# A sine by polynomial on GpSimd, and VectorE's steps around the first two scans in a written order

## The chip, the cores and the metric

The kernel runs on one core of a Trainium2 chip: TensorE (PE in the rows), VectorE (DVE), ScalarE (ACT), GpSimd (POOL) and the SyncE queue (SP) that issues the loads. The metric is the device time of one execution in microseconds (us); the median of three executions counts.

## What is computed

A two-layer block over `x` of 16 sequences of 256 tokens and 256 features. Layer 0 is a layer norm, a diagonal complex recurrence (32 states) over time, and a GELU perceptron whose output gates it:

```python
mag, theta = exp(-exp(softplus(nu_log))), exp(theta_log)
A = mag * (cos(theta) + i sin(theta)); gamma = sqrt(1 - mag * mag)
h[t] = A * h[t-1] + gamma * (B @ xn[t])            # complex, 32 states
s = Re(C @ h) + D * xn
g = silu(proj2 @ gelu(proj1 @ xn + b1) + b2)       # 256 -> 1024 -> 256
x = x + s * g
```

Layer 1 is causal attention with a low-rank key and value path and 16 heads, gated by a mixture of LoRA experts. The change lies in layer 0 alone.

## The kernel before

Layer 0 takes the tokens in eight chunks of 512 (`NC = 8`, chunk `c`). The five engines have programs of their own, written as loops over 70 steps `g` (`L0_STEPS`), and what stands in a step is a hand-written table of step numbers; semaphores alone order one engine against another. A step of TensorE has one up block, hidden block `g`: `l0_up` (six products of 512 columns into one of two banks `fbank`), and the down block of two steps before, `l0_down(g-2)` (twelve products of 256 columns). Numbers are split in a high and a low part, so every product stands three times (`three`, line 537). Between lie, once in a chunk: `l0_turn` (transposes of the normed input `xn`, two halves), `l0_bu` (the recurrence's input), and `l0_y(c, b)` (line 597, the product of the states `Z[b]` with the matrix `RR`).

ScalarE does the high parts: `x_high`, `w1_high`, `w2_high`, `b_high`, and in each step `l0_gelu` (gelu of the bank into `hs`, then a rounded copy `hh`). VectorE does the low parts (`x_low`, `w1_low`, `w2_low`, `b_low`, and `h_low`, which writes `hl`), the layer norm (`l0_stats`, `l0_normed`; the first two chunks' roots too, `l0_norm`), the size of the decay (`magnitude`, a chain of one-column steps handed out by `go(make, 7)`), and `scan(c)`: the input is turned by tables `tci`, `tsi` (four steps), summed, scanned in time, and turned back by `tc`, `tsn` (the two halves of `CS`) into `Z[0]` and `Z[1]`. `states_out` adds the product of `l0_y` to the skip path, `l0_sum` and `l0_gate` make the gate, `l0_out` writes `x`.

GpSimd makes the tables: it exponentiates `theta_log`, reduces eight angles (1, 2, 4 ... 128 times theta), gives them halved to ScalarE (semaphore `ang`), which takes the sine (`angles`), then fixes the pairs to length one and doubles the table `CS` eight times. It then scales `RR`, `tci` and `tsi`, fills the small tables `rope_c`, `rope_s`, and takes the roots of later chunks (`l0_roots`) and two products on weights of layer 1 (`weigh_factors`, line 1951).

The places the change touches: ScalarE's start (lines 1079 to 1128), where an up block's gelu stands behind three `w1_high` and `angles`; TensorE's `l0_up(0)` and the tables of `l0_bu`, `l0_turn`, `l0_y` (lines 807 to 845); VectorE's loop (lines 1653 to 1756); GpSimd's table maker (lines 1866 to 1915).

Of the kernel before, what the change touches and what calls it, by code (L numbers as in the profile page):

```python
# [59 lines left out]
PRODUCT_AT = 5  # L60
L0_STEPS = 70
# [11 lines left out]
    "w1h", "w2h", "bh", "xth", "gelu", "hsh", "sin", "th0", "wrh", "wnh", "wmh", "lbh", "woh",  # L73
    "yth", "mi", "kt", "qn", "gx", "mt", "th1", "p", "oth",
# [5 lines left out]
    "gated", "clean", "par", "ang", "nu", "tab", "rt", "fill", "rl", "lr", "kr", "kvr", "n", "qq", "nw", "rs", "oc", "kwk", "kwv",  # L80
# [110 lines left out]
def build(nc, x, consts, rows, vecs, w1t, w2t, b1c, bt, ct, nuth, wqn, wkbt, wqr, wkva, wvbt, wo,  # L191
          baset, lorab, loraa, routert, out):
    ctx = ExitStack()
    with ctx:
# [60 lines left out]
        pari = sb("pari", [128, 4], I32, l0)  # L255
        st0 = sb("st0", [128, 4, 6], F32, l0)
# [95 lines left out]
        top = lg[:, 96:112].rearrange("p (t x) -> p t x", t=2)  # L352

# [178 lines left out]
        def _(e):  # L532
# [24 lines left out]

            def l0_up(c, hb):
# [38 lines left out]
            def l0_y(c, b):  # L597
                w.wait_ge("zz", 2 * c + b + 1)
# [191 lines left out]
            for g in range(L0_STEPS):  # L790
# [43 lines left out]
                c, r = divmod(g - 4, 8)  # L834
                if r == 0 and 0 <= c < NC - 1:
                    l0_turn(c + 1, 0)
# [6 lines left out]
                if g in (11, 16, 23, 31, 39, 47, 55, 63):  # L843
                    c = (11, 16, 23, 31, 39, 47, 55, 63).index(g)
                    l0_y(c, 1)
# [51 lines left out]
        def _(e):  # L897
# [39 lines left out]
            def angles():  # L937
                w.wait_ge("ang", 1)
                w.wait_ge("sin", 1)
                e.activation(col(48, 16), col(32, 16), ACT.Sin).then_inc(SEM["sin"], 1)  # L940
# [6 lines left out]
            def rope_high():  # L947
                w.wait_ge("wqr", 16)
                for k in range(2):
                    e.activation(wq_hi[:, k, :, 128:256], wrs[:, k, :, :], ACT.Copy,  # L950
                                 scale=-SCALE).then_inc(SEM["wrh"], 1)
# [128 lines left out]
            e.activation(col(56), tsn[:, 0:1], ACT.Sin).then_inc(SEM["sin"], 1)  # L1080
# [3 lines left out]
            for g in range(L0_STEPS):  # L1084
                c, r = divmod(g - 10, 8)
                if r == 0 and 0 <= c < NC:
                    l0_tanh(c, 0)
                c, r = divmod(g - 10, 8)
                if r == 0 and 0 <= c < NC:
# [7 lines left out]
                if g == 3:  # L1097
                    b_high()
                if g == 0:
                    w1_high(1)  # L1100
                if g == 0:
                    w1_high(2)
                if g == 0:
                    w1_high(3)
# [4 lines left out]
                if g == 0:  # L1109
                    angles()  # L1110
                if g == 1:
                    w2_high(0)
                if g == 2:
                    w2_high(1)
                if g == 3:
                    w2_high(2)
                if g == 5:
                    w2_high(3)
# [8 lines left out]
                if g == 11:  # L1127
                    rope_high()
                if g == 64:
                    weighed(0)  # L1130
                if g < 8 * NC:
                    l0_gelu(g)
                if g == 54:
# [12 lines left out]
                c, r = divmod(g - 4, 8)  # L1146
                if r == 0 and 0 <= c < NC - 1:
# [60 lines left out]
        def _(e):  # L1208
# [30 lines left out]
            def l0_stats(c):  # L1239
                w.wait_ge(f"x{c}", 16)  # L1240
                w.wait_ge("xn", c)
                for i in range(4):
                    if c == 0 and i == 2:
                        w.wait_ge("x0b", 16)
                    j = e.bn_stats(st0[:, i, :], X[:, 4 * c + i, :])
                j.then_inc(SEM["bn"], 1)
                took("bn")
                for i in range(4):
                    j = e.bn_aggr(mv0[:, i, :], st0[:, i, :])
# [3 lines left out]
            def l0_normed(c):  # L1253
                if c > 1:
                    w.wait_ge("rl", c - 1)
                w.wait_ge("xo", 2 * (c - 2))
                for i in range(4):
                    j = e.tensor_scalar(xn[c % 3][:, i, :], X[:, 4 * c + i, :], mv0[:, i, 0:1], rs0[:, 4, i:i + 1],
# [13 lines left out]
            def magnitude():  # L1272
# [40 lines left out]
                e.tensor_tensor(gamma, gamma, t[:, 4, :], ALU.mult).then_inc(SEM["mag"], 1)  # L1313
# [43 lines left out]
            def scan(c):  # L1357

                w.wait_ge("bu", c + 1)
                w.wait_ge("tab", 3)  # L1360
# [61 lines left out]
            def rope_low():  # L1422
                for k in range(2):
                    w.wait_ge("wrh", k + 1)
                    e.scalar_tensor_tensor(wq_lo[:, k, :, 128:256], wrs[:, k, :, :], -SCALE,
                                           wq_hi[:, k, :, 128:256].bitcast(F32), ALU.mult,
                                           ALU.subtract).then_inc(SEM["wrl"], 1)
# [224 lines left out]
            gate = norm = make = iter(())  # L1652
            for g in range(L0_STEPS):
                c, r = divmod(g - 3, 8)
                if r == 0 and 1 <= c < NC - 1:
                    l0_normed(c + 1)
                c, r = divmod(g - 0, 8)
# [5 lines left out]
                if g == 1:  # L1663
                    w2_low(0)
                if g == 2:
                    w2_low(1)
                if g == 3:
                    w2_low(2)
                if g == 6:
                    w2_low(3)  # L1670
                if g == 58:
                    l1_kv(0)
                if g in (7, 13, 21, 29, 37, 45, 53, 61):
                    c = (7, 13, 21, 29, 37, 45, 53, 61).index(g)
                    skip(c, 0)
                if g in (10, 16, 23, 31, 39, 47, 55, 63):
                    c = (10, 16, 23, 31, 39, 47, 55, 63).index(g)
                    skip(c, 1)
                if g == 0:
                    w1_low(1)  # L1680
                if g == 0:
                    w1_low(2)
                if g == 0:
                    w1_low(3)
                if g in (9, 12, 20, 28, 36, 44, 52, 60):
                    c = (9, 12, 20, 28, 36, 44, 52, 60).index(g)
# [13 lines left out]
                if g == 11:  # L1700
                    rope_low()
# [13 lines left out]
                if g == 4:  # L1715
# [4 lines left out]
                if g == 4:  # L1720
# [473 lines left out]
```

## Time and profile before

| What | us |
|---|---|
| median of three executions (796.82 to 797.35) | 797.14 |
| the profiled execution's own time | 797.71 |
| its span | 795.9 |
| PE busy in the span | 780.1 |
| DVE busy | 682.7 |
| ACT busy | 524.0 |
| POOL busy | 477.1 |

The span is the time from the first to the last instruction on the core; the profiled execution's own time is 1.8 us more. Busy time is a sum over the whole span. A stretch of TensorE's busy time can be at either of its two granted clocks (1.2 or 2.4 GHz), which the rows by stretch give as a share of the higher (PEclk).

### The profile page before, as it was taken

The numbers are of one execution on the slowest core, as the hardware profiler recorded it, in microseconds if no ns is written. First come the engines' busy times: TensorE is split into PE (matmuls) and PEld (weight loads), VectorE is DVE, ScalarE is ACT, GpSimd is POOL, SyncE is SP. The second block draws the span as 40 slices with busy tenths as digits, with TensorE's granted clock in tenths as the row PEclk, the third lists the DMA queues.
The fourth block names the chain that finished last, engine by engine and source line by source line (L and its number), as shares of the span: only waits on it lengthen the run. The fifth ranks groups of instructions, "written<-read, shape, count | busy, mean of one in ns | idle before, by whom it ended". The sixth has DMA issues, their size and how long they took to land.

```text
span 795.9 us, 23134 instructions
## 1 busy us (share of the span) xinstructions
PE 780.1 (98%) x7976; PEld 712.7 (90%) x7976; DVE 682.7 (86%) x2615; ACT 524.0 (66%) x1612; POOL 477.1 (60%) x1261
## 2 busy tenths in 40 slices
PE   7999999999999999999999999999999999999988
PEld 5888888888889889899988999999899998999867
DVE  6898797887788799899898998988899998999885
ACT  4554455455563787777767777777777767777682
POOL 6833022022334687776868677686776868668673
PEclk8999999999999999999999999999999999999999
DMA  8600011000001322232222322222232222322120
GB/s 297 251 20 18 1 68 67 1 1 1 1 12 33 55 46 44 55 63 39 52 39 44 56 54 54 38 47 46 54 65 34 49 42 50 57 47 52 33 52 28
DMA packets 101334, 41.15 MB, mean 52 GB/s; under 512 B 91744, under 2 KB 98400, under 8 KB 100576
## 3 DMA queue, kind: packets, MB, share of 16 engines
q1 hardware_dynamic: 98896, 38.89, 21.9%
q8 instruction: 63, 1.03, 0.5%
q10 hardware_dynamic: 2320, 0.79, 0.4%
q14 instruction: 55, 0.45, 0.2%
HBM read 14.47 MB, written 4.19 MB: 23 GB/s over the span
## 4 chain that ended last, share of the span: by engine, by line
PE 88%; DVE 5%; POOL 2%; issue 2%; ACT 2%; ACTq 0%; DMA 0%; POOLq 0%; DVEq 0%
PE bank L537 61%; PE bank L745 11%; PE bank L767 8%; PE bank L738 3%; PE bank L601 1%; POOL par L1822 1%; DVE SM L1583 1%; PE bank L653 1%; ACT SM L1036 1%; PE bank L554 1%; DVE PT L1606 1%; PE bank L613 1%; PE bank L627 1%; POOL SM L1989 1%; PE bank L672 0%
## 5 line engine op out<-in xcount | busy, mean ns | idle before, releaser
L1036 ACT ACTIVATE SM<-SM,stb 128x224 f32<-128x224 f32 (+7 forms) x512 | 206.1, 405 | 63.4 <-DVE stb L1583 58.9
L1989 POOL TENSOR_SCALAR SM<-SM,stb 128x224 f32<-128x224 f32 (+7 forms) x512 | 196.1, 402 | 67.0 <-DVE stb L1590 65.5
L537 PE MATMUL bank<-yh,wq_lo 128*128 128x256 f32 x512 | 150.5, 294 | 0.0
L537 PE MATMUL bank<-yh,wq_hi 128*128 128x256 f32 x512 | 144.6, 282 | 0.0
L537 PE MATMUL bank<-yl,wq_hi 128*128 128x256 f32 x512 | 144.6, 282 | 0.0
L745 PE MATMUL bank<-KT,QT 128*128 128x192 f32 (+4 forms) x640 | 120.9, 327 | 1.7 <-DVE stb L1583 1.7
L1583 DVE CUSTOM_DVE_ANT_0 SM<-bank,CONST 128x224 f32<-128x224 f32 (+3 forms) x320 | 96.9, 346 | 24.1 <-PE bank L745 21.3
L1606 DVE STREAM_TRANSPOSE PT<-SM 128x128 f32<-128x128 f32 (+2 forms) x232 | 99.4, 460 | 16.2 <-PE bank L767 16.2
L745 PEld LDWEIGHTS bank<-KT,QT 128*128 128x128 f32 x640 | 97.5, 190 | 5.3 <-DVE stb L1583 3.6
L537 PEld LDWEIGHTS bank<-yh,wq_lo 128*128 128x128 f32 x512 | 97.0, 190 | 1.4
L537 PEld LDWEIGHTS bank<-yh,wq_hi 128*128 128x128 f32 x512 | 97.0, 190 | 0.0
L537 PEld LDWEIGHTS bank<-yl,wq_hi 128*128 128x128 f32 x512 | 97.0, 189 | 0.0
L1036 ACT ACTIVATION_READ_ACCUMULATOR SM<-SM,stb 128x1 f32 x512 | 96.1, 188 | 0.0
L921 ACT ACTIVATE hs<-bank,B 128x512 f32<-128x512 f32 x64 | 43.9, 686 | 74.1 <-PE bank L537 68.6
L1982 POOL TENSOR_TENSOR QA<-QA 128x256 f32<-128x256 f32 x62 | 46.3, 746 | 58.5 <-DVE QA L1554 58.5
L1008 ACT ACTIVATE QT<-bank 64x512 f32<-64x512 f32 x128 | 75.4, 589 | 6.5 <-PE bank L537 4.8
L1554 DVE TENSOR_TENSOR QA<-bank,TR 128x512 f32<-128x512 f32 x124 | 79.3, 682 | 0.2
L537 PE MATMUL bank<-woe_hi,ol 128*128 128x256 f32 x256 | 75.4, 294 | 0.7 <-issue 0.7
L537 PE MATMUL bank<-w2h,hl 128*128 128x256 f32 x256 | 74.4, 291 | 0.0
L537 PE MATMUL bank<-w2l,hh 128*128 128x256 f32 x256 | 72.4, 283 | 0.0
L537 PE MATMUL bank<-w2h,hh 128*128 128x256 f32 x256 | 72.4, 283 | 0.0
L537 PE MATMUL bank<-woe_hi,oh 128*128 128x256 f32 x256 | 72.1, 281 | 0.0
(218 smaller groups left out, 2068.9 us busy)
## 6 DMA issues: line engine op xcount, KB each, us to landing
QT<-QA SPq DMA_DIRECT2D x240, 64.0 KB, 2.1
PT<-KV SPq DMA_DIRECT2D x256, 16.0 KB, 1.8
out<-fo SPq DMA_DIRECT2D x32, 128.0 KB, 2.0
X<-in_x SPq DMA_DIRECT2D x7, 512.0 KB, 11.2
stage<-in_wqn SPq DMA_DIRECT2D x2, 1024.0 KB, 9.2
stage<-in_wo SPq DMA_DIRECT2D x2, 1024.0 KB, 5.0
stage<-in_w1t SPq DMA_DIRECT2D x4, 256.0 KB, 5.6
stage<-in_w2t SPq DMA_DIRECT2D x2, 512.0 KB, 7.6
```

The source lines that it names most:

```text
L537: i = e.matmul(dst, a, b, start=(first and j == 0), stop=(last and j == 2), skip_group_check=skip)
L738: j = e.matmul(sbank[n % 2][32 * i:32 * i + 32, at:to], KT[b % 3][:, p, 32 * kb:32 * kb + 32], Q[:, :, kb:3, i, :], start=True, stop=True)
L745: j = e.matmul(sbank[n % 2][:, at], Q[:, q, :, :].rearrange("p h c -> p (h c)"), KT[b % 3][:, p, 0:32 * q + 32], start=True, stop=True)
L767: j = e.matmul(sums[64 * half:64 * half + 64, :, 32 * q:32 * end], C[rows_, kb // 2, at], PT[rows_, 2 * half:2 * half + 2, kb, q:end, :], ...
L921: e.activation(hs[g % 2][:, :], fbank[g % 2][:, :], ACT.Gelu, bias=B1[:, g % 8:g % 8 + 1]).then_inc(SEM["gelu"], 1)
L1008: i = e.activation(QT[r, (2 * b + g // 2) % 3, p, :, g % 2:4:2, :].rearrange("p n j c -> p j n c"), src[r, :, :, :], ACT.Copy)
L1036: i = e.activation(M[:, at], M[:, at], ACT.Exp, bias=S[:, 0, j:j + 1], scale=-1.0, accum_out=S[:, 1, j:j + 1])
L1554: i = e.tensor_tensor(A[:, part, :, :, g % 2, :], src, TR[:, part, :].rearrange("p (n c) -> p n c", n=8).unsqueeze(1).broadcast_to([128, 2 ...
L1583: i = e.tensor_tensor_reduce(M[:, at], bk[:, at], mask[:, 224 - 32 * q:256], 1.0, 3e38, ALU.add, ALU.min, S[:, 0, j:j + 1])
L1606: return e.transpose(PT[:, slot, 0:k, q:q + some, :].rearrange("p k q c -> p q k c"), src)
L1982: e.tensor_tensor(A[:, 0, 0, :, :], A[:, 0, 0, :, :], A[:, 1, 1, :, :], ALU.subtract)
L1989: i = e.tensor_scalar(P[:, at], P[:, at], S[:, 2, j:j + 1], 1.0, ALU.mult, ALU.mult)
```

## The change

It does six things. (1) ScalarE no longer takes the sine. GpSimd evaluates sine and cosine of the half angles by polynomials of the squared angle, two of eight columns at once, in 15 instructions where it had nine, and without a wait for ScalarE; ScalarE's first instruction is a gelu of one column instead of a sine. (2) `w1_high` and `w1_low` of parts 1 to 3 are spread over steps (0, 2, 4 on ScalarE, 0, 2, 5 on VectorE) instead of standing all in step 0; `w2_low`, `b_high`, `b_low` move by a step or two. (3) TensorE's first up block takes its products with the input's high part first and those with the low part last. (4) ScalarE makes `tci` and `tsi` after gelu 10; GpSimd's `rope` tables move behind the roots of chunk 2. (5) VectorE's steps 10 to 18 are written out in one function, and the steps of TensorE for the first two chunks' states move: `l0_bu(0)` from step 5 to 7 and `l0_bu(1)` from 12 to 14, `l0_y` from steps 10, 11, 14, 16 to 12, 13, 16, 17, all four behind the down block. (6) Chunk 3's statistics use layer 1's small buffers, so that they can be taken in step 10 (before: 16); `rope_high` and `rope_low` are split, and the latter moves from step 11 to 20 and 22.

```diff
+TURN_FIRST = (5, 13, 20, 28, 36, 44, 52)
+BU_AT = (7, 14, 20, 28, 36, 44, 52, 60)
+SCAN_AT = (10, 14, 20, 28, 36, 44, 52, 60)
+Y_AHEAD = {8 * c + 6: c for c in range(2, NC)}
+Y_BEHIND = {12: (0, 0), 13: (0, 1), 16: (1, 0), 17: (1, 1), **{8 * c + 7: (c, 1) for c in range(2, NC)}}
...
+            def l0_first():
+                sl = slice(0, 128)
...
+                for k in range(2):
+                    w.wait_ge("xth", k + 1)
+                    e.matmul(fbank[0][:, :], w1l[:, k, sl], xh[0][:, k, :], start=(k == 0), stop=False)
+                    e.matmul(fbank[0][:, :], w1h[:, k, sl], xh[0][:, k, :], start=False, stop=False)
+                for k in range(2):
+                    w.wait_ge("xtl", k + 1)
+                    i = e.matmul(fbank[0][:, :], w1h[:, k, sl], xl[0][:, k, :], start=False, stop=(k == 1))
...
+            def rotated_tables():
+                w.wait_ge("cs", 1)
+                w.wait_ge("mag", 1)
+                e.activation(tci[:, :], tc, ACT.Copy, scale=col(6)).then_inc(SEM["tab"], 1)
+                e.activation(tsi[:, :], tsn, ACT.Copy, scale=col(7)).then_inc(SEM["tab"], 1)
...
-            e.activation(col(56), tsn[:, 0:1], ACT.Sin).then_inc(SEM["sin"], 1)
+            e.activation(trig[:, 15, 0:1], tsn[:, 0:1], ACT.Gelu)
...
+            def first_steps(g):
+                if g == 10:
+                    l0_stats(3)
+                if g in (12, 13, 16, 18):
+                    states_out(*{12: (0, 0), 13: (0, 1), 16: (1, 0), 18: (1, 1)}[g])
+                if g == 14:
+                    l0_gate(0, 1)
+                if g == 17:
+                    l0_sum(1)
+                h_low(g)
+                if g == 10:
+                    go(make)
+                    scan(0)
+                if g == 11:
+                    l0_normed(2)
...
+                if g == 13:
+                    l0_gate(0, 0)
+                    x_low(2, 0)
+                if g == 14:
+                    x_low(2, 1)
+                    scan(1)
...
-            w.wait_ge("sin", 2)
-            tt(c8, c8, c8, ALU.mult)
...
+            ts(ab, r8, 0.5, None, ALU.mult)
+            both = ab.unsqueeze(1).broadcast_to([128, 2, 8])
+            tt(q1.rearrange("p (i n) -> p i n", i=2), both, both, ALU.mult)
+            tt(SUMS[:, 0:3, :], ODD, q1.unsqueeze(1).broadcast_to([128, 3, 16]), ALU.mult)
...
+            e.tensor_tensor(CS[:, :, 128:256], CS[:, :, 128:256], G[:, :, 0:128], ALU.add).then_inc(SEM["cs"], 1)
```

ScalarE at its start, before (`xh0` is the input's high part, `hs` and `hh` the gelu's output and its rounded copy, `stage` the loaded weights):

```order
L1080 ACT_TABLE_LOAD
L1080 ACTIVATE par<-CS 128x1 [waits par]
L903 ACTIVATE w1h<-stage0 128x2x256 [waits wu0]
L914 ACTIVATE xh0<-bank 128x512 [waits tx] x2
L903 ACTIVATE w1h<-stage0 128x2x256 [waits wu1]
L903 ACTIVATE w1h<-stage0 128x2x256 [waits wu2]
L903 ACTIVATE w1h<-stage0 128x2x256 [waits wu3]
L940 ACTIVATE par<-par 128x16 [waits sin,ang]
L921 ACT_TABLE_LOAD [waits b1]
L921 ACTIVATE hs0<-bank,B1 128x512 [waits f1]
```

The same place in the change:

```order
L1109 ACT_TABLE_LOAD
L1109 ACTIVATE trig<-CS 128x1 [waits par]
L932 ACTIVATE w1h<-stage0 128x2x256 [waits wu0]
L943 ACTIVATE xh0<-bank 128x512 [waits tx] x2
L932 ACTIVATE w1h<-stage0 128x2x256 [waits wu1]
L950 ACTIVATE hs0<-bank,B1 128x512 [waits b1,f1]
L954 ACTIVATE hh0<-hs0 128x512 [waits gelu]
L937 ACTIVATE w2h<-stage1 128x512 [waits wd0]
L950 ACTIVATE hs1<-bank,B1 128x512 [waits f1]
```

Two loads of weights, the sine and a second table load no longer stand ahead of the first gelu.

VectorE ahead of the first scan, before (`st0` holds the statistics of chunk 2, `hl` is the low part of a gelu's output, `G` the turned input):

```order
L1354 TENSOR_TENSOR hl1<-hs1,hh1 128x512 [waits f2,hsh,gelu]
L1245 BN_STATS st0<-X 128x6 [waits xn,x2]
L1245 BN_STATS st0<-X 128x6 x3
L1249 BN_AGGR mv0<-st0 128x2 [waits bn]
L1249 BN_AGGR mv0<-st0 128x2 x3
L1354 TENSOR_TENSOR hl2<-hs0,hh2 128x512 [waits f2,hsh,gelu]
L1366 TENSOR_TENSOR G<-bank,tci 64x256 [waits mag,tab,bu]
```

And in the change (`z0` is the sum of a chunk's down blocks, `st1` holds the statistics of chunk 3):

```order
L1428 TENSOR_TENSOR z0<-bank,VEC0 128x512 [waits f2]
L1428 TENSOR_TENSOR z0<-bank,VEC0 128x512
L1380 TENSOR_TENSOR hl0<-hs1,hh0 128x512 [waits hsh,gelu]
L1267 BN_STATS st1<-X 128x6 [waits x3]
L1267 BN_STATS st1<-X 128x6 x3
L1271 BN_AGGR mv1<-st1 128x2 [waits bn]
L1271 BN_AGGR mv1<-st1 128x2 x3
L1380 TENSOR_TENSOR hl1<-hs0,hh1 128x512 [waits hsh,gelu]
L1392 TENSOR_TENSOR G<-bank,tci 64x256 [waits mag,tab,bu]
```

The scan moves behind the sum of the first chunk's down blocks, the statistics of chunk 3 and the low part of step 10; before, the sum stood behind the scan and those statistics six steps later.

VectorE ahead of the second chunk's normed input `xn1`, before (`w1l` is a low part of weights, `mv0` what the root's steps start from):

```order
L1319 TENSOR_TENSOR w1l<-stage0,w1h 128x2x256 [waits wu1,w1h]
L1319 TENSOR_TENSOR w1l<-stage0,w1h 128x2x256 [waits wu2,w1h]
L1319 TENSOR_TENSOR w1l<-stage0,w1h 128x2x256 [waits wu3,w1h]
L1245 BN_STATS st0<-X 128x6 [waits xn,x1]
L1245 BN_STATS st0<-X 128x6 x3
L1249 BN_AGGR mv0<-st0 128x2 [waits bn]
L1249 BN_AGGR mv0<-st0 128x2 x3
L1220 TENSOR_SCALAR rs0<-mv0 128x4 [waits bn]
```

And in the change:

```order
L1380 TENSOR_TENSOR hl1<-hs1,hh1 128x512 [waits hsh,gelu]
L1345 TENSOR_TENSOR w1l<-stage0,w1h 128x2x256 [waits wu2,w1h]
L1267 BN_STATS st0<-X 128x6 [waits xn,x1]
L1267 BN_STATS st0<-X 128x6 x3
L1271 BN_AGGR mv0<-st0 128x2 [waits bn]
L1271 BN_AGGR mv0<-st0 128x2 x3
L1380 TENSOR_TENSOR hl2<-hs0,hh2 128x512 [waits hsh,gelu,bn]
L1352 TENSOR_TENSOR w2l<-stage1,w2h 128x512 [waits w2h]
L1240 TENSOR_SCALAR rs0<-mv0 128x4
```

Before, the statistics stood ahead of every `hl`; now the `hl` of steps 0 and 1 come before them and that of step 2 right behind. In both, the root's twelve steps follow, broken by one more `hl`, and then `xn1`; the last `w1l` now comes two steps after `xn1`.

## Rows read from the trace of the kernel before

**Rows 1.** The page: busy time, share of the span and instructions of each engine.

```profile
PE 780.1 (98%) x7976; PEld 712.7 (90%) x7976; DVE 682.7 (86%) x2615; ACT 524.0 (66%) x1612; POOL 477.1 (60%) x1261
```

**Rows 2.** Stretches: us, busy of each engine, PEclk, DMA share, GB/s.

```profile
11.00:14.40 3.40, 2.88 (x7) 2.33 (x8) 2.26 (x4) 1.52 (x4) 2.78 (x8) 0.50 1.05 389
14.40:17.80 3.40, 1.44 (x7) 0.86 (x5) 2.90 (x13) 2.52 (x4) 2.54 (x10) 1.00 1.05 412
17.80:21.20 3.40, 3.26 (x9) 2.71 (x10) 2.87 (x12) 3.20 (x6) 2.80 (x8) 0.51 1.02 413
```

**Rows 3.** Timeline of PE: start, us, instruction, in brackets the idle time before.

```profile
11.52 0.77 PE L537 MATMUL bank<-xh,w1l 128*128 128x512 f32 x1 [1.14 <-DVE xl L1347]
...
17.94 0.76 PE L537 MATMUL bank<-xh,w1l 128*128 128x512 f32 x1 [2.10 <-ACT hs L921]
18.50 0.63 PE L537 MATMUL bank<-xl,w1h 128*128 128x512 f32 x1
18.93 0.63 PE L537 MATMUL bank<-xh,w1h 128*128 128x512 f32 x1
...
21.27 0.28 PE L537 MATMUL bank<-w2h,hl 128*128 128x256 f32 x1
...
44.30 0.40 PE L537 MATMUL bank<-xh,w1l 128*128 128x512 f32 x1
...
46.25 1.13 PE L601 MATMUL bank<-RR,Z 128*128 128x256 f32 x4 [0.39 <-DVE Z L1378]
...
63.01 0.63 PE L554 MATMUL bank<-CONST,xn 128*128 128x128 f32 x4 [0.82 <-DVE xl L1347]
```

**Rows 4.** Timeline of ACT, 9 to 18 us.

```profile
9.99 1.08 ACT L914 ACTIVATE xh<-bank 128x512 fp32r<-128x512 f32 x2 [3.36 <-PE bank L554]
...
14.10 0.63 ACT L903 ACTIVATE w1h<-stage 128x512 fp32r<-128x512 f32 x1 [1.41 <-DMA stage<-in_w1t]
15.58 0.22 ACT L940 ACTIVATE par<-par 128x16 f32<-128x16 f32 x1 [0.85 <-POOL par L1880]
15.81 1.28 ACT L921 ACT_TABLE_LOAD   x1
17.11 0.69 ACT L921 ACTIVATE hs<-bank,B 128x512 f32<-128x512 f32 x1
17.83 0.63 ACT L925 ACTIVATE hh<-hs 128x512 fp32r<-128x512 f32 x1
```

**Rows 5.** Groups of DVE, 10 to 50 us: count, busy us, mean ns, idle before.

```profile
L1354 DVE TENSOR_TENSOR hl<-hs,hh 128x512 fp32r<-128x512 f32 x10 | 7.2, 722 | 3.1 <-ACT hs L921 2.0 <-issue 0.8 <-ACT hh L925 0.3
L1245 DVE BATCH_NORM_STATS2 st<-X 128x6 f32<-128x256 f32 x8 | 2.8, 410 | 0.0
L1249 DVE BATCH_NORM_AGGREGATE mv<-st 128x2 f32<-128x6 f32 x8 | 0.8, 157 | 0.1
L1231 DVE TENSOR_TENSOR rs<-rs 128x4 f32<-128x4 f32 x3 | 0.5, 162 | 0.1
L1258 DVE TENSOR_SCALAR xn<-X,mv,rs 128x256 f32<-128x256 f32 x4 | 1.4, 404 | 0.0
```

**Rows 6.** Timeline of DVE: the low input, the first scan's ends, a slow step.

```profile
10.69 1.29 DVE L1347 TENSOR_TENSOR xl<-bank,xh 128x512 fp32r<-128x512 f32 x2 [0.63 <-ACT xh L914]
...
42.35 0.41 DVE L1366 TENSOR_TENSOR G<-bank,tci 64x256 f32<-64x256 f32 x1
...
46.66 0.42 DVE L1378 TENSOR_TENSOR Z<-gs,CS 64x256 f32<-64x256 f32 x1
...
78.54 2.36 DVE L1258 TENSOR_SCALAR xn<-X,mv,rs 128x256 f32<-128x256 f32 x4
```

**Rows 7.** Timeline of POOL: ends of the table's chain, and the weights' products.

```profile
15.62 1.18 POOL L1822 TENSOR_SCALAR par<-par 128x1 f32<-128x1 f32 x4
...
38.43 0.74 POOL L1828 TENSOR_TENSOR CS<-CS,G 128x256 f32<-128x256 f32 x1
...
76.33 3.46 POOL L1951 TENSOR_TENSOR stk<-stk,VEC 128x512 f32<-128x512 f32 x2
```

More of the change, by code:

```diff
@@ L1108, in _ @@
                     y_high(0, wbank)
[L1109 to L1118, printed above, removed]
+                if g in (1, 3, 5, 6):
+                    w2_high((1, 3, 5, 6).index(g))
                 if g == 38:
@@ L1132, in _ @@
                     l0_gelu(g)
+                if g == 10:
+                    rotated_tables()
+                if g in (10, 18):
+                    for half in range(2):
+                        l0_tanh((g - 10) // 8, half)
+                if g in (11, 12):
+                    rope_high(g - 11)
                 if g == 54:
@@ L1253, in l0_normed @@
             def l0_normed(c):
+                _, means, roots, _ = norm_buffers(c)
                 if c > 1:
@@ L1312, in magnitude @@
                 yield from rsqrt("mg", gamma, 0.0, t, pari[:, 3:4])
-                e.tensor_tensor(gamma, gamma, t[:, 4, :], ALU.mult).then_inc(SEM["mag"], 1)
+                e.tensor_tensor(gamma, gamma, t[:, 4, :], ALU.mult).then_inc(chain, 1)
+                took("mg")
+                w.wait_ge("const", 16)
+                e.tensor_tensor(col(7), gamma, sgn, ALU.mult).then_inc(SEM["mag"], 1)
             def w1_low(n):
@@ L1420, in l0_out, with rope_low @@
                                        ALU.add).then_inc(SEM["xo"], 1)
[L1422 to L1427, printed above, removed]
+            def rope_low(k):
+                w.wait_ge("wrh", k + 1)
+                e.scalar_tensor_tensor(wq_lo[:, k, :, 128:256], wrs[:, k, :, :], -SCALE,
+                                       wq_hi[:, k, :, 128:256].bitcast(F32), ALU.mult,
+                                       ALU.subtract).then_inc(SEM["wrl"], 1)
             def nope_low(g, k):
@@ L1863, in _ @@
             done[0] += 1
+            ODD, EVEN, SUMS, PAIRS = (trig[:, i:i + n, :] for i, n in ((0, 3), (3, 3), (6, 4), (10, 2)))
+            q1, q2, q4 = (trig[:, i, :] for i in (12, 13, 14))
+            for k in range(7):
+                at = SUMS[:, 3, :] if k == 6 else (ODD if k % 2 else EVEN)[:, k // 2, :]
+                e.memset(at[:, 0:8], float((-1) ** k / math.factorial(2 * k + 1)))
+                i = e.memset(at[:, 8:16], float((-1) ** k / math.factorial(2 * k)))
+            i.then_inc(SEM["par"], 1)
+            done[0] += 1
             w.wait_ge("nuth", 16)
@@ L1925, in l0_roots @@
             def l0_roots(c):
-                full, a, y0, half, y = (rs0[:, i, :] for i in range(5))
+                _, means, roots, guess = norm_buffers(c)
+                full, a, y0, half, y = (roots[:, i, :] for i in range(5))
                 w.wait_ge("bn", 2 * c + 2)
-                w.wait_ge("xn", c)
-                then(e.tensor_scalar(full, mv0[:, :, 1], LN_EPS, None, ALU.add))
+                if c != 3:
+                    w.wait_ge("xn", c)
+                then(e.tensor_scalar(full, means[:, :, 1], LN_EPS, None, ALU.add))
                 then(e.tensor_scalar(half, full, -0.5, None, ALU.mult))
-                then(e.tensor_scalar(ri0[:, :], full.bitcast(I32), -0.5, 1597463007.0, ALU.mult, ALU.add))
-                src = ri0[:, :].bitcast(F32)
+                then(e.tensor_scalar(guess[:, :], full.bitcast(I32), -0.5, 1597463007.0, ALU.mult, ALU.add))
+                src = guess[:, :].bitcast(F32)
                 for dst in (y0, full, y):
```

222 lines of the change are left out of this document (111 added, 111 removed).

## The prediction

> **What bounds the kernel now.** I read the page first: TensorE is busy in 98% of the span, VectorE in 86%, the other two in two thirds or less [rows 1]. So only what TensorE waits for, or does at its lower clock, can be won, some 16 us in all. The timeline of TensorE shows where its waits lie in layer 0: 1.14 us for VectorE's `xl` before the first product, 2.10 us for a gelu before up(2) at 17.94, 0.39 us for the first states at 46.25, 0.82 us for `xl` at 63.01 [rows 3]. The stretches show the clock: 0.50 of full from 11.0 to 14.4, full from 14.4 to 17.8, 0.51 from 17.8 to 21.2, and between the two slow stretches TensorE was busy only 1.44 of 3.40 us [rows 2]. A product of 512 columns then starts 0.43 us after the one before (18.50, 18.93), and the first after a wait 0.56 (17.94 to 18.50) [rows 3]. At the higher clock I take half, 0.22, and half of that for 256 columns.
>
> The wait of 2.10 us is ScalarE's: it waited 1.41 us for the last quarter of weights, then 0.85 for GpSimd's angles, took the sine at 15.58, and loaded another table for 1.28 us; the first gelu began at 17.11 [rows 4]. Ahead of it nothing else was missing.
>
> **Part 1: the start, -4.4 us.** The first up block now needs only the input's high part. ScalarE's two steps from 9.99 take 1.08 us, so the first is done at 10.55 [rows 4]; VectorE's first `xl` was done at 11.38 and TensorE began at 11.52, 0.14 later [rows 3, 6]. So the first product starts at 10.7. The products with the low part stand last and are not waited for: by then `xl` is done (11.98 [rows 6]). I leave the slow clock from 11.0 to 14.4 in place. Then up(0), six products, ends at 13.2; up(1) does three at 0.43 and three at 0.22 and ends at 15.1. The gelu of block 0 runs from 13.4 to 14.1 (0.69, and 0.63 for its copy [rows 4]), so up(2), which waits for that gelu, follows at once and ends at 16.5. Down(0) needs `hl` of block 0 (15.5) and the low weights `w2l`, two steps of 0.7 later (16.2). Its fourth product starts at 16.9; before it started at 21.27 [rows 3]. That is -4.4, of which 2.1 is the wait, 1.7 the second slow stretch (3.4 us at half the pace [rows 2]), the rest the earlier start. The weights' last quarter landed at 14.1 [rows 4] and is now taken behind gelu 3; the spread of `w1_high` costs nothing as long as TensorE reaches up(6), which needs it, after VectorE has done `w1l`, near 27.
>
> **Part 2: a new wait for `xn1`, +0.4 us.** TensorE's first transposes of chunk 1 stand behind up(5): 16.9, then 1.0 for the rest of down(0), three up blocks and two down blocks at 1.35, so 24.7. VectorE has, from the copy of gelu 1 (16.7, the gelu standing behind `w2_high`) on: two `hl`, one part each of `w1l` and `w2l`, of the size of an `hl`, another `hl`, five in all at 0.72; the statistics, 1.4 and 0.4; twelve root steps at 0.16 to 0.2, 2.2; `xn1`, 1.4 [rows 5]. The sum is 9.0, less 0.6 for what neighbours overlap: 25.1, or 25.5 if they do not. Bounds 0 and 0.8; I take 0.4.
>
> **Part 3: the two states' waits, -1.5 us.** 0.39 and 0.82 go [rows 3], with 0.13 each for the first product after a wait (0.56 less 0.43): -1.5. For the first: with parts 1 and 2, up(10) starts at 40.4 instead of 44.30 [rows 3], and `l0_y(0, 0)` now stands behind three up and three down blocks, at 48.8. VectorE, from down(7)'s end at 40.5, does the sum (1.3), `hl` (0.65), statistics (1.8), `hl` (0.65) and begins the scan at 44.9; it took 4.7 us to the end of its last step, 3.85 to the first pair [rows 6], so `Z[0]` is there at 48.75. The margin is nothing, but a late scan costs only what it is late. For the second, the transposes wait for `xl` of chunk 2, which now stands ahead of the scan.
>
> **Part 4: GpSimd's tables, 0.** After the clamp GpSimd has 14 steps of the exponential, 15 of the polynomial, 32 of the doubling, 61; before there were 55, from 15.62 to 39.17 (38.43 + 0.74), so 0.43 each, with all that VectorE did beside them [rows 7]. One step earlier and 61 at 0.43: `CS` at 41.3. ScalarE takes it behind the copy of gelu 10, at 43.1, two steps of under half a microsecond. The scan at 44.9 covers them. If that cover is gone, a later table costs its lateness in full, since the scan, `l0_y` and, on ScalarE, gelu 11 stand behind it. `RR`, the chunk's roots and the `rope` tables follow on GpSimd with 3 us and more to spare.
>
> **Part 5: moved steps, +0.4 us.** `weigh_factors` used to run at 76.33, in 3.46 us, and beside it VectorE's normed input took 2.36 instead of 1.4 us [rows 5, 6, 7]. GpSimd now reaches them near 55, beside `xl` of chunk 2, on which transposes wait with no margin. Bounds 0 and 1.1 (the growth of that one step and a tenth); I take 0.4, as two of VectorE's seven steps there lie on the path. `rope_low`, two steps of 1.2 us, goes behind step 20; SP's loads of `wm` behind it come some 30 us later and are wanted at step 26, 10 us after they land: 0. SP's reload of `stage` waits for the last `w1l`, 12 us later than before, and is wanted from step 18 on: 0.
>
> **The rest** is in the order of before, and TensorE bound; I carry the gain through. The sum: -4.4 + 0.4 - 1.5 + 0.4 = **-5.1 us**. The profiled execution took 797.71, so 792.6; it stands 0.57 above the median of 797.14, which gives **792.0**.
>
> **The rivals.** *The clock does not fall.* TensorE idles less before 11.0, and if it keeps the higher clock the slow 3.4 us cost 1.7 less; VectorE's chain of part 2 moves less than TensorE, so 0.4 of it comes back: -6.4, 790.7. Against it: the wait for the normed input remains, and what TensorE does in between is transposes. The Trainium skill (TensorE: Matmul & The Clock Gate, Part 4) says that transposes do not count as busy in the way other matmuls do; by that rule the clock falls here as before. I give it 0.15.
>
> *VectorE becomes the bound.* Every place named above without margin is VectorE's. With part 2 at its upper end (+0.4), part 5 too (+0.7), and 0.6 at the first scan: -3.4, 793.7. Chance 0.15.
>
> *GpSimd's table is late by some us.* `CS` decides from 44.0 on, two short steps of ScalarE before the scan. At 0.55 us for each of the 61 steps, between the 0.43 they took and the 0.72 of a whole `hl` of VectorE [rows 5, 7], it is there at 48.7, 4.7 late: 796.7, about the old time. For it: GpSimd's neighbour VectorE did slow down once beside it, to 2.36 us [rows 6]. The Trainium skill (SBUF — State Buffer, Who interferes with whom) says that a VectorE step with two SBUF inputs and a GpSimd step that reads SBUF exclude each other for a whole step; those 2.36 us agree in kind. Against it: `hl` stood beside the 55 steps too and is in their 0.43. Chance 0.04.
>
> *Slower.* The same mechanism, further on: ScalarE stands at `rotated_tables`, with gelu 11 and so up(13) behind it, and each us of `CS` after 44.0 costs one. Slower by more than 0.2% needs 5.1 + 1.6 of them, `CS` at 50.7, so 0.58 us for each of 61 steps; at 0.6, `CS` at 51.7, it is 799.7. For it: the new steps are up to 48 columns wide; against it: doublings of up to 256 columns are in the 0.43. Chance 0.03.
>
> *It does not do what it says*: some wait of layer 0's end, hidden so far, gives the gain back. The order there is unchanged, and TensorE is busy throughout; 0.02, at 796.5.
>
> **How the numbers follow.** Forecast 0.61, clock 0.15, VectorE 0.15, tables late 0.04, slower 0.03, given back 0.02. A measurement can tell about 0.2%, 1.6 us, from no change. Faster by that: 0.61 + 0.15 + 0.15 = 0.91; within: 0.06; slower: 0.03. The range takes in the clock and no new wait (-4.4 - 1.7 - 1.5 + 0.4: 789.9) and, above, VectorE's bounds with half a microsecond for the tables: 794.6.
>
> **What would show it.** The first product at 10.7, the gelu of block 0 near 13.4 with no table load, no wait over 0.5 us before up(2), full clock from 14.4 on; up(10) near 40.4; `CS` near 41 and ScalarE not standing before `tci`; the first states' product without a wait near 49; TensorE's idle time down by some 4 us. It is wrong if a slow stretch reappears after 14.4, if ScalarE stands for GpSimd before step 11, or if layer 1 shows new waits.

## The result and the profile after

The changed kernel takes 791.58 us (median of six executions, 791.52 to 791.67), the kernel before 797.59 beside it (796.82 to 798.18): a ratio of 0.9925, with a 95% interval of 0.9914 to 0.9935. The profiled executions stand at 791.67 and 797.71, spans 789.9 and 795.9. So 6.0 us are gone, where 5.1 were forecast.

The page, busy time of each engine, as in [rows 1]: TensorE has the same products and is busy 1.5 us less. That is a net sum: the two stretches at half clock are gone, and the 24 products ahead of the first transposes take 8.45 us in this execution, where they took 6.92.

```profile
PE 778.6 (99%) x7976; PEld 711.5 (90%) x7976; DVE 681.7 (86%) x2616; ACT 524.5 (66%) x1612; POOL 479.5 (61%) x1278
```

The stretches of [rows 2] in the changed kernel, in the same columns, with the one ahead of them:

```profile
7.60:11.00 3.40, 3.06 (x19) 2.57 (x18) 2.52 (x8) 0.91 (x2) 2.62 (x9) 1.00 0.95 303
11.00:14.40 3.40, 3.40 (x15) 2.51 (x15) 1.95 (x4) 2.39 (x5) 2.55 (x11) 1.00 1.01 360
14.40:17.80 3.40, 3.20 (x21) 2.60 (x20) 2.93 (x7) 3.34 (x7) 2.84 (x7) 1.00 1.04 421
17.80:21.20 3.40, 3.40 (x22) 3.06 (x21) 3.19 (x15) 2.13 (x4) 2.83 (x8) 1.00 1.02 412
```

The granted clock is full in all four; before, two of the last three had half. TensorE is busy 13.06 of 13.60 us. The first of these stretches in the kernel before:

```profile
7.60:11.00 3.40, 1.80 (x11) 0.92 (x9) 2.67 (x9) 1.01 (x3) 2.64 (x8) 1.00 0.86 282
```

Timeline of PE, the places of [rows 3] (start, us, instruction, in brackets the idle time before):

```profile
10.84 0.47 PE L578 MATMUL bank<-xh,w1l 128*128 128x512 f32 x1 [0.34 <-ACT xh L943]
...
13.86 0.39 PE L549 MATMUL bank<-xh,w1l 128*128 128x512 f32 x1
...
15.57 0.36 PE L549 MATMUL bank<-w2h,hl 128*128 128x256 f32 x1 [0.20 <-DVE w2l L1352]
...
24.59 0.66 PE L566 MATMUL bank<-CONST,xn 128*128 128x128 f32 x4 [0.32 <-DVE xn L1281]
...
48.20 1.02 PE L629 MATMUL bank<-RR,Z 128*128 128x256 f32 x4
...
56.03 0.63 PE L566 MATMUL bank<-CONST,xn 128*128 128x128 f32 x4
```

The first product, up(2), down(0), the transposes of chunk 1, the first states' product and the second transposes of chunk 2. Of the old waits (1.14, 2.10, 0.39, 0.82) the first is 0.34 and the others are gone; 0.20 and 0.32 are new. Followed along the program, TensorE's lead is 4.08 us at up(2), 5.26 at up(4), 4.56 from up(8) to up(10), and 6.12 from up(19) on; at the end it is 6.04. So layer 1 gives back less than 0.1 us in this execution.

Timeline of ACT, as [rows 4], with the steps of `rotated_tables` (L965, L966):

```profile
10.09 1.09 ACT L943 ACTIVATE xh<-bank 128x512 fp32r<-128x512 f32 x2 [3.20 <-PE bank L566]
11.07 0.63 ACT L932 ACTIVATE w1h<-stage 128x512 fp32r<-128x512 f32 x1
12.68 0.69 ACT L950 ACTIVATE hs<-bank,B 128x512 f32<-128x512 f32 x1 [0.97 <-PE bank L582]
...
42.59 0.49 ACT L965 ACTIVATE tci<-CS,par 128x256 f32<-128x256 f32 x1
42.99 0.50 ACT L966 ACTIVATE tsi<-CS,par 128x256 f32<-128x256 f32 x1
```

The first gelu waits for its own up block now, not for a load, an angle or a table. `tci` follows the copy of gelu 10 without a wait: the last step of `CS` on GpSimd had ended 1.32 us before:

```profile
40.53 0.74 POOL L1962 TENSOR_TENSOR CS<-CS,G 128x256 f32<-128x256 f32 x1
```

### The profile page after: what moved, and what is told of

The parts are those of the page before. It is cut to its first block, busy times and chain, and to the rows that moved or that the text cites. A ratio compares the mean times of both kernels' runs of the same rounds, so it can differ in the third digit from the quotient of the medians.

```text
span 789.9 us, 23152 instructions
## 1 busy us (share of the span) xinstructions
PE 778.6 (99%) x7976; PEld 711.5 (90%) x7976; DVE 681.7 (86%) x2616; ACT 524.5 (66%) x1612; POOL 479.5 (61%) x1278
## 4 chain that ended last, share of the span: by engine, by line
PE 92%; DVE 4%; ACT 1%; POOL 1%; issue 1%; ACTq 0%; POOLq 0%; DVEq 0%
PE bank L549 63%; PE bank L773 11%; PE bank L795 8%; PE bank L766 3%; PE bank L629 2%; PE bank L815 1%; PE bank L566 1%; DVE SM L1608 1%; PE bank L681 1%; ACT SM L1065 1%; DVE PT L1631 1%; PE bank L641 1%; PE bank L655 1%; POOL SM L2051 1%; PE bank L700 0%
```

## The experiments

Each but the ninth is the changed kernel with the edit shown, beside fresh executions of the kernel before on the same chip. "TensorE's lag" is the start of a block against the changed kernel's own profile (the first one, 791.67).

**1. Is the gain steady?** The changed kernel unaltered.

> The changed kernel itself, unaltered, timed again beside the others. Theory (its waits at the start are too short for TensorE's clock to fall): all executions within 0.3 us of 791.6. Rival (the clock's fall is chance, and the executions so far had luck): some executions 1.6 to 3 us above, as the kernel with the weights taken early and the one with the low part in its old place showed.

791.60 us (791.41 to 792.27), ratio 0.9931 (0.9919 to 0.9944). The theory holds, nearly: one execution is 0.67 above, none 1.6. The profile has full clock from 5.2 us to the end of the work.

**2. The weights early again.**

```diff
-                if g in (0, 2, 4):
-                    w1_high(1 + g // 2)
+                if g == 0:
+                    w1_high(1)
+                    w1_high(2)
+                    w1_high(3)
```

(and `w1_low` of parts 1 to 3 all in step 0)

> The changed kernel with one part undone: ScalarE takes the high parts of the first layer's weights 1 to 3 all ahead of gelu 0, and VectorE their low parts all in step 0, as before; the polynomial stays. Theory (the gain at the start is what stands ahead of gelu 0): gelu 0 waits for the last quarter of weights, landed near 13.5 to 14, and begins at 14.1 to 14.7 instead of 12.68; up(2) follows it some 1.4 us later; 792.6 to 793.2 us, and if TensorE's clock falls in the wait, 1.6 more. Rival (the sine alone held the gelu; the order of the weights is worth nothing): 791.6 us within 0.3.

793.84 us (791.60 to 796.45, eleven executions), ratio 0.9960 (0.9949 to 0.9971). In the profile, at 793.37 and at full clock, gelu 0 begins at 14.28, up(2) after a wait of 1.18 at 15.09; TensorE lags by 1.19 us from up(8) on and by 1.67 from up(19) on. So the order of the weights is worth 1.2 us directly; the other 0.5 goes near 67 and 72 us, with 0.17 of it a listed wait for `z`. The median lies 0.6 above the theory's range, and why the executions spread over 5 us one profile can't say.

**3. The sine's wait and table back, the polynomial kept.**

```diff
-            e.activation(trig[:, 15, 0:1], tsn[:, 0:1], ACT.Gelu)
+            e.activation(trig[:, 15, 0:1], tsn[:, 0:1], ACT.Sin)
...
+                if g == 0:
+                    w.wait_ge("ang", 1)
+                    e.activation(trig[:, 15, 8:16], col(40, 8), ACT.Sin).then_inc(SEM["sin"], 1)
```

> The changed kernel, GpSimd's polynomial kept, with ScalarE's old work ahead of gelu 0 added: it starts with the sine's table, waits for GpSimd's angles, takes a sine of 8 columns into a scratch tile (not used) and loads the gelu's table. Theory: the angles come near 16, the table takes 1.28 us, gelu 0 begins near 17.4 instead of 12.68, and 4.2 to 4.7 us of it arrive at the end: 795.8 to 796.3 us, with 1.6 more if the clock falls: up to 797.9. Rival (the order of the products and of the weights carries the gain, the sine is hidden): under 793 us. Rival (the gain is chance of the clock): 793.2, that is 1.6 more and no wait.

796.44 us (796.25 to 796.94), ratio 0.9990 (0.9981 to 0.9999). Timeline of ACT in this kernel:

```profile
14.49 0.21 ACT L1146 ACTIVATE trig<-par 128x8 f32<-128x8 f32 x1 [2.90 <-POOL par L1938]
14.71 1.28 ACT L950 ACT_TABLE_LOAD   x1
16.01 0.69 ACT L950 ACTIVATE hs<-bank,B 128x512 f32<-128x512 f32 x1
```

The angles came earlier than I expected, and gelu 0 is 3.33 late. TensorE waits 2.93 before up(2), its clock is half from 17.8 to 21.2, and it lags by 2.98 at up(2), 4.37 at up(3) and 4.00 from up(8) on. Then a loss comes that I had not put down to the sine, 1.08 us at the second transposes of chunk 2. Timelines of PE, DVE and POOL in this kernel:

```profile
61.20 0.63 PE L566 MATMUL bank<-CONST,xn 128*128 128x128 f32 x4 [1.08 <-DVE xl L1376]
```

```profile
58.00 1.85 DVE L1383 TENSOR_TENSOR hl<-hs,hh 128x512 fp32r<-128x512 f32 x1
...
60.37 0.68 DVE L1376 TENSOR_TENSOR xl<-bank,xh 128x512 fp32r<-128x512 f32 x1
```

```profile
56.76 2.54 POOL L2018 TENSOR_TENSOR stk<-stk,VEC 128x512 f32<-128x512 f32 x2
```

`hl` takes 1.85 us instead of 0.68, beside GpSimd's two weight products.

**4. The same with those products cut** to one column in 64; the other columns are left out.

```diff
-                e.tensor_tensor(f, f, kw, ALU.mult).then_inc(SEM[what], 1)
+                n = 1 if what == "kwk" else 64
+                e.tensor_tensor(f[:, :, 0:n], f[:, :, 0:n], kw[:, :, 0:n], ALU.mult).then_inc(SEM[what], 1)
```

> The kernel with the sine put back on ScalarE, and GpSimd's two products on layer 1's weights cut from 64 to 1 column of each of 8 groups (the rest of those products is left out, so layer 1's keys differ). Theory (hl took 1.85 us there because a product ran beside it, and that made xl late by 1.08): hl takes 0.7, no wait before the transposes near 61, 795.1 to 795.4 us instead of 796.44. Rival (something else makes xl late, the order of VectorE's steps): 796.3 to 796.6 as before.

795.46 us (795.19 to 796.80), ratio 0.9977 (0.9968 to 0.9986). DVE and PE in the same place:

```profile
57.79 0.68 DVE L1383 TENSOR_TENSOR hl<-hs,hh 128x512 fp32r<-128x512 f32 x1
```

```profile
59.82 0.63 PE L566 MATMUL bank<-CONST,xn 128*128 128x128 f32 x4
```

`hl` is back at 0.68, the wait is gone, and 0.98 us of the median come back. The products made `xl` late.

**5. The old order of the first products** (`l0_up(0)` for `l0_first`).

```diff
-                if g == 0:
-                    l0_first()
-                elif g < 8 * NC:
+                if g < 8 * NC:
```

> The changed kernel with the first up block in the old order of products: a low-part product second. Theory: the first products run up to xl (near 11.4 to 12), up(0) ends 0.4 to 0.7 us later; of that VectorE's wait before down(0) and that for xn1 take up some, since they are set by VectorE: 791.7 to 792.2 us. Rival (TensorE's start sets the end in full): 792.3. Rival (the clock falls after such a wait as before): 1.6 more, 793.3 to 793.9.

792.72 us (792.23 to 795.59), ratio 0.9953 (0.9939 to 0.9967). The wait of 1.14 for `xl` is back; TensorE lags by 0.73 at up(0) and 0.59 from up(8) on. The waits for `w2l` and `xn1` are still there, 0.22 and 0.34. So the rival that TensorE's start sets the end holds: VectorE's chain follows the gelus, these follow the up blocks, and a later start shifts all of them. Four executions lie at 792.2 to 793.2, two at 795.1 and 795.6; the profile shows one of the four, 793.17, at full clock, although the same 1.14 us stand in it as in [rows 3]. That execution lost 0.8 us more in layer 1, where VectorE stood 1.84 us for a transfer and TensorE then 0.53 for VectorE:

```profile
306.26 1.29 DVE L1577 TENSOR_TENSOR QA<-bank,TR 128x512 f32<-128x512 f32 x2 [1.84 <-DMA QT<-QA]
```

```profile
307.70 0.36 PE L549 MATMUL bank<-wm_hi,yl 128*128 128x256 f32 x1 [0.53 <-DVE QA L1577]
```

The changed kernel's profile has neither wait. Without it the lag of 0.59 fits the three executions at 792.23 to 792.28.

**6. All three undone together**, so that only the written-out steps stay.

> All three undone together (weights early, sine's wait and table on ScalarE, low part in the old place); what is left of the change is the written-out order of VectorE's steps and the moved products of the states. Theory (the parts add: the states' two waits are worth 1.5 us by themselves): 796.0 to 796.5 us, with the clock falling twice as in the kernel before. Rival (the states' waits are gone only because VectorE got ahead; without the early start they come back): 797.3 to 797.9. Rival (the sum of the single losses): over 798.

796.69 us (795.76 to 797.75), ratio 0.9993 (0.9985 to 1.0002): of the 6 us nothing that this measurement can tell from zero. The wait for the first states is gone, that for `xl` stands again with 1.01 us, for the reason of run 3. Here it is the step on `z` that stretches (1.79, with two SBUF inputs like `hl`), beside the products from 56.44 to 59.52:

```profile
58.28 1.79 DVE L1438 SCALAR_TENSOR_TENSOR z<-th,z 128x512 f32<-128x512 f32 x1
```

The gelu of block 0 begins at 16.77 and TensorE waits 3.15 us for it, at full clock ahead of the wait and behind it.

**7. The new start alone**: VectorE's steps 9 to 18 and TensorE's tables as before.

```diff
-BU_AT = (7, 14, 20, 28, 36, 44, 52, 60)
-SCAN_AT = (10, 14, 20, 28, 36, 44, 52, 60)
+BU_AT = (5, 12, 20, 28, 36, 44, 52, 60)
+SCAN_AT = (9, 12, 20, 28, 36, 44, 52, 60)
...
-                if 10 <= g < 19:
-                    first_steps(g)
-                    continue
```

(and `l0_y` in steps 10, 11, 14, 16, `b_high` and `b_low` in 3 and 4, `rotated_tables` behind gelu 9)

> The changed kernel with its new start (polynomial, spread weights, high-part products first), but with VectorE's steps 9 to 18 and TensorE's steps for the states and the transposes as before, and with the rotated tables behind gelu 9. Theory (the early start pays only because the first states' product stands later): the table is ready near 41.3, the scan starts near 42.2 and Z is there near 46, but the product of the states stands behind up(10), which ends near 41; TensorE waits some 4 to 5 us: 796 to 797.5 us, so nearly the whole gain is given back. Rival (the parts add: only the states' 1.5 us are lost): 793.1 us.

799.73 us (798.93 to 800.16), ratio 1.0029 (1.0018 to 1.0041): slower than the kernel before. Timelines of POOL, ACT and PE in this kernel:

```profile
41.29 0.72 POOL L1956 TENSOR_TENSOR CS<-CS,G 128x256 f32<-128x256 f32 x1
```

```profile
42.05 0.51 ACT L963 ACTIVATE tci<-CS,par 128x256 f32<-128x256 f32 x1 [2.02 <-POOL CS L1956]
```

```profile
41.07 0.39 PE L549 MATMUL bank<-xh,w1h 128*128 128x512 f32 x1
47.03 2.04 PE L629 MATMUL bank<-RR,Z 128*128 128x256 f32 x4 [5.58 <-DVE Z L1402]
```

and the stretch from the wait's end on:

```profile
45.30:52.20 6.90, 5.17 (x18) 4.74 (x19) 6.77 (x13) 1.23 (x2) 4.58 (x15) 0.51 0.01 2
```

TensorE comes to the states' product 5 us before the table lets them be made, waits 5.58 us, and then works 5.17 at half clock, which costs half of that, 2.6. Together 8.2, and the profiled execution is 8.1 above the changed kernel (799.81 against 791.67). I had the wait right and left out the clock.

**8. GpSimd's products 3.5 us earlier** (the `rope` tables behind them).

```diff
-                if g == 9:
-                    rope_tables()
...
                     weigh_factors("kwk", 1)
+                    rope_tables()
```

> The changed kernel with GpSimd's rope tables moved from ahead of the roots of chunk 3 to behind the two products on layer 1's weights, so that these begin near 54.5 instead of 57.4. Theory (a VectorE step with two SBUF inputs stands still while such a product runs, as the 1.85 us of hl in the kernel with the sine put back suggest; the change was lucky by two microseconds): one of hl or z stretches to 1.5 to 2 us, xl of chunk 2 is late, TensorE waits near 1 us before a transpose: 792.3 to 792.8 us. Rival (TensorE's order covers it, no wait): 791.6 within 0.2.

791.70 us in the median, but in two groups: four executions at 791.36 to 791.74, two at 794.02 and 795.38; ratio 0.9942 (0.9926 to 0.9958). The profile is of the one at 795.38. Timelines of DVE, POOL and PE:

```profile
54.02 1.73 DVE L1380 TENSOR_TENSOR hl<-hs,hh 128x512 fp32r<-128x512 f32 x1
55.66 1.76 DVE L1435 SCALAR_TENSOR_TENSOR z<-th,z 128x512 f32<-128x512 f32 x1
57.35 0.68 DVE L1373 TENSOR_TENSOR xl<-bank,xh 128x512 fp32r<-128x512 f32 x1
```

```profile
53.90 2.98 POOL L2013 TENSOR_TENSOR stk<-stk,VEC 128x512 f32<-128x512 f32 x2
```

```profile
58.17 0.87 PE L566 MATMUL bank<-CONST,xn 128*128 128x128 f32 x4 [2.04 <-DVE xl L1373]
```

`hl` and `z` stretch beside the two products, and the lag is 3.68 us, of which 2.04 is the wait and the rest a stretch at half clock behind it:

```profile
58.40:61.80 3.40, 3.40 (x17) 3.33 (x16) 2.84 (x7) 0.60 (x1) 1.15 (x3) 0.50 0.01 2
```

So the theory's mechanism is there, and larger than the 1 us I gave it. Four executions escape and lie about where the rival had them. They may differ in how the products fall against `hl`, but no profile of one of them was taken, so that is not shown.

**9. The kernel before, profiled again**, for its clock.

> The kernel before, one look, for its clock. Theory (the fall of TensorE's clock near 11 us is hidden behind the gelu that the angles set, that near 18 us is not): the first gelu begins within 0.3 us of 17.1 whether or not the clock fell ahead of it, and the time is 796.6 to 798.1 with the second fall, near 796 without. Rival (each stretch costs 1.6): 794.5 to 795 without a fall.

797.36 us, a single execution. Its stretches:

```profile
11.70:15.10 3.40, 3.39 (x8) 2.72 (x9) 2.46 (x5) 1.22 (x3) 2.79 (x7) 0.50 1.05 394
15.10:18.50 3.40, 1.93 (x8) 1.28 (x8) 2.67 (x15) 3.05 (x5) 2.45 (x11) 0.99 1.03 416
18.50:21.90 3.40, 2.91 (x19) 2.35 (x18) 3.19 (x10) 3.34 (x7) 2.94 (x7) 1.00 1.01 405
```

The first fall is there, the second is not, and the time is only 0.35 us shorter, where the theory had 796. The gelu of block 0 begins at 16.92, against 17.11 [rows 4], since the angles come at 15.39 against 15.58: the first fall is hidden behind the angles in both. Where TensorE is quicker after that, it meets VectorE, 0.49 us for `w2l` before down(0). From up(2) to up(3) it takes 3.61 us with this wait and 4.40 in the first profile, so 0.79 is left of the stretch's price, and TensorE is 0.80 ahead of the first profile from up(19) until 297 us, in layer 1. It then loses 0.46, at full clock, at the place that run 5 showed (VectorE stands 1.50 us for a transfer):

```profile
312.00 0.36 PE L537 MATMUL bank<-wm_hi,yl 128*128 128x256 f32 x1 [0.22 <-DVE QA L1554]
```

In run 6 gelu 0 is at 16.77 with no fall at all.

**10. Three further versions.** (a) The first quarter of the second layer's weights one step earlier, into ScalarE's idle 0.97 us:

```diff
-                if g in (1, 3, 5, 6):
-                    w2_high((1, 3, 5, 6).index(g))
+                if g in (0, 3, 5, 6):
+                    w2_high((0, 3, 5, 6).index(g))
```

(and `w2_low(0)` behind `w1_low(1)` in step 0)

> The changed kernel with the first quarter of the second layer's weights taken one step earlier, ahead of gelu 0 on ScalarE (it stands idle there for 0.97 us) and ahead of the first hl on VectorE (idle for 1.45 us). Theory: the wait of 0.20 us before down(0) goes, and since VectorE's chain comes 0.5 us earlier the one of 0.32 for xn1 too, with what the first product after a wait costs: 790.9 to 791.3 us. Rival (gelu 0 is pushed back by the load): 791.6 to 792.

791.29 us (791.06 to 791.35), ratio 0.9925 (0.9913 to 0.9937). The wait for `w2l` is gone, the one for `xn1` is not (0.38): TensorE moved up as far as VectorE did.

(b) The same with TensorE's transposes of chunk 1 behind the down block of step 5.

> The kernel with the second layer's first weights taken early, and TensorE's first transposes of chunk 1 put behind the down block of step 5 instead of ahead of it. Theory (xn1 is 0.38 late there and nobody needs the transposes before up(8)): the wait goes, 790.8 to 791.0 us instead of 791.29. Rival (ScalarE's and VectorE's steps on the transposed input come later and delay hl and so a down block): 791.3 to 791.8.

791.29 us (791.22 to 791.39), ratio 0.9919 (0.9905 to 0.9932): nothing. The wait moved on to 0.19 us before the second transposes, for `xl`, and 0.16 before `l0_bu(0)`, for `bl` (the low part of `B`). VectorE was the limit, not the place of the wait.

(c) Version (a) with the first layer's third quarter early too: `w1_high(2)` ahead of gelu 0, `w1_low(2)` ahead of the first `hl`.

> The kernel with the second layer's first weights taken early, and the first layer's third quarter too: ScalarE's high part of it stands ahead of gelu 0 and VectorE's low part ahead of the first hl, where VectorE still idles 0.85 us. Theory (VectorE's chain, not TensorE's order, sets the 0.38 us for xn1): the chain from hl 1 to xn1 loses one step of 0.6, the wait goes, 790.7 to 791.0 us instead of 791.29. Rival (that quarter lands too late and pushes gelu 0 back): 791.4 to 792.

790.75 us (790.55 to 791.41), ratio 0.9912 (0.9899 to 0.9926). ScalarE's `w1h` ends as gelu 0 becomes ready, and VectorE's step stands where it idled:

```profile
11.98 0.63 ACT L932 ACTIVATE w1h<-stage 128x512 fp32r<-128x512 f32 x1
12.55 0.69 ACT L950 ACTIVATE hs<-bank,B 128x512 f32<-128x512 f32 x1
```

```profile
13.09 0.68 DVE L1347 TENSOR_TENSOR w1l<-stage,w1h 128x512 fp32r<-128x512 f32 x1
14.01 0.69 DVE L1382 TENSOR_TENSOR hl<-hs,hh 128x512 fp32r<-128x512 f32 x1 [0.24 <-ACT hh L954]
```

The waits view lists none for TensorE between the first product and 204 us. This is the fastest version measured: 0.8 us below the changed kernel by the medians, and 0.93 ahead of it at the end of the two profiles. The intervals of the two ratios still overlap.

## Why the prediction was right, and where it was not

The forecast was 792.0, the median is 791.58. The direction, the size and the place of most of it were right; three terms were mis-sized: parts 1 and 5 came out better by 0.86 and 0.4, part 2 worse by 0.3. The sum in the profiled executions is 6.04 instead of 5.1. (The upper end of the range was added up wrongly: its terms give 794.2, not 794.6. Nothing rests on it.)

**Part 1, the start: -4.4 forecast, -5.26 measured** at the fourth product of down(0) (16.01, before 21.27). The step that failed is "I leave the slow clock from 11.0 to 14.4 in place". It did not fall, so the rival that I gave 0.15 is what happened. up(0) and up(1) took 3.0 us instead of 4.4, gelu 0 began at 12.68 and not at 13.4. What TensorE did ahead of that place, before the change and in run 3:

```profile
8.87 0.44 PE L554 MATMUL bank<-CONST,xn 128*128 128x128 f32 x2 [0.78 <-DVE xn L1258]
9.51 0.87 PE L554 MATMUL bank<-CONST,xn 128*128 128x128 f32 x6 [0.21 <-DVE xn L1258]
```

```profile
8.86 0.44 PE L566 MATMUL bank<-CONST,xn 128*128 128x128 f32 x2 [0.78 <-DVE xn L1284]
9.51 0.88 PE L566 MATMUL bank<-CONST,xn 128*128 128x128 f32 x6 [0.21 <-DVE xn L1284]
10.73 0.47 PE L578 MATMUL bank<-xh,w1l 128*128 128x512 f32 x1 [0.34 <-ACT xh L943]
```

The waits for the normed input are 0.78 and 0.21 us in both; only the third differs, 1.14 [rows 3] and 0.34. The clock fell in the first and stayed full in run 3, from 10.70 on:

```profile
10.70:14.10 3.40, 3.18 (x12) 2.05 (x12) 1.87 (x3) 0.89 (x2) 2.63 (x10) 1.00 1.03 367
```

Run 7 has 0.73, 0.21 and 0.34, and no fall there either; the second profile of the kernel before has 0.60, 0.21 and 1.14, and it fell. So the shorter third wait goes with the clock that stays. It is not the whole cause: in runs 5 and 6 1.14 us stand behind a single wait of 0.21, and the clock stays full.

TensorE's 3.06 us of busy time from 7.6 to 11.0 in the changed kernel's own profile, against 1.80 before, are in part no doing of the change, since the 24 products ahead of the transposes happened to end at 9.62 there instead of 8.09.

The rule of the Trainium skill that I set against this rival (TensorE: Matmul & The Clock Gate, Part 4) would have had the clock fall with transposes between such waits; in run 3 they stand from 8.86 to 10.39 between waits of 0.78, 0.21 and 0.34 and the clock stays, so as I applied it the trace does not agree.

The split of the -4.4 was off too. "1.7 the second slow stretch" was too much: without that stretch TensorE's way from up(2) to up(3) is 0.79 us shorter (run 9), because VectorE's `w2l` is next. What the start owes, runs 2, 3 and 5 show: undone one at a time, 1.19 us of TensorE's lag for the weights, 4.00 for the sine, 0.59 for the order of the products. Together, undone at once (run 6), 3.69 from up(8) to up(13), less than for the sine alone, since the clock fell in run 3 and not in run 6. The sine and the weights are two waits ahead of one gelu, and taking away only one of them leaves the other.

**Part 2, the wait for `xn1`: +0.4 forecast**, between 0 and 0.8. The wait is 0.32, and with the slower products behind it up(5) to up(6) takes 3.79 us instead of 3.25: 0.54. A further 0.16 is lost at `l0_bu(0)`, whose first product starts at 31.22, 0.15 after VectorE's `bl` ends; I had not seen that place. Together 0.70 from up(4) to up(8). That VectorE's chain ends the wait for `xn1` was right, as version (c) shows.

**Part 3, the states' waits: -1.5 forecast, -1.56 measured** (from 4.56 to 6.12). `Z[0]`'s two steps end at 47.90 and TensorE comes at 48.20: a margin of 0.3 us. The words "the two states' waits" were too wide, though: the second is a wait for `xl`, and it went only because part 5 cost nothing.

**Part 4, GpSimd's tables: 0 forecast, 0 measured.** `CS` was put at 41.3 and ends at 41.27, and ScalarE did not stand for it. The cover is what run 7 takes away: with the scan in its old step ScalarE waits 2.02 us for `CS` and TensorE 5.58. The rival "slower" named this place, and what kept it off is the written order of steps 10 to 18. Its price, a microsecond for each that the table is late, is not shown: no run made the table later in the changed order, and run 7, which moved the scan, paid 2.6 us of half clock on top of the wait.

**Part 5, moved steps: +0.4 forecast, 0 measured**, with 1.1 as the upper end. That was luck of timing. I had put the products near 55; they run from 57.40 to 59.95 in the changed kernel:

```profile
57.40 2.55 POOL L2013 TENSOR_TENSOR stk<-stk,VEC 128x512 f32<-128x512 f32 x2
```

`xl`, which TensorE waits for, ends at 55.88, and beside the products VectorE does steps that read the bank and one SBUF input, at their usual 0.41 to 0.69 us. Runs 3 and 6 show that the upper end is real, waits of 1.08 and 1.01 us, and run 8 goes beyond it with 2.04, once the products begin earlier against VectorE's steps. The Trainium skill (SBUF — State Buffer, Who interferes with whom) says that a VectorE step with two SBUF inputs and a GpSimd step that reads SBUF exclude each other; `hl` at 1.73 to 1.85, `z` at 1.76 and 1.79, and the untouched `xl` and `G` agree with it.

**The parts do not add.** The new steps alone (run 6) are worth 0.5 us by the medians, with an interval that takes in zero; the new start alone (run 7) costs 2.3 us against the kernel before, by its ratio; both give 6.0. The sum by parts came out since each was worked out with the other in place.

## What to carry to other kernels

Before a start is made earlier, ask what will then be the first thing that TensorE finds missing, and when that is ready at the earliest: here the states' table, at 41 to 42 us whatever the start, so that 5 us of lead turned into a wait of 5.58 until the product that needs it was placed later. Where several waits end at one instruction, undoing or removing one of them tells little; price them together. And a gain with a margin of 0.3 us, as at `Z[0]`, or of 2 us, as between `z`, the last step ahead of `xl` with two SBUF inputs (it ends at 55.28), and GpSimd's products at 57.40, is one that the next edit can lose, as runs 3, 6 and 8 did.

## What had not been expected of the hardware

The granted clock does not follow the length of a single wait in these profiles. It fell from full to half in or behind waits of 2.93 (run 3), 2.94 (run 4), 2.04 (run 8) and 5.58 us (run 7). In the kernel before it fell behind 0.78, 0.21 and 1.14 with transposes between, and again behind 2.10. It did not fall around 3.15 us in run 6, around 1.47 before up(2) in run 9, around 1.18 in run 2, nor around 1.14 in runs 5 and 6. The 24 products ahead of the first transposes, the same in every kernel here, took between 6.91 and 8.49 us, since the clock first rose anywhere between 4.2 and 7.4 us. What decides when it falls is left open.

Executions of one kernel also lie apart. In run 8 the profile of a long execution shows where 3.68 us went; of the longest executions of runs 2 and 5 no profile was taken. In runs 5 and 9 part of a microsecond goes to a transfer of layer 1 that landed late, near 307 and 312 us, so that two profiles can differ by 0.5 to 0.8 us at a place that no edit touched.
